# Attention scores as 64-query by 128-key products on quarters of the TensorE array, and a rearranged state-space stage (norm a turn ahead, B and C projected once, mask as a product)

## The reference

```python
x = x + ssd_block(layernorm(x))          # first stage: state-space attention in chunks, 4 heads of 64
x = x + layers(layernorm(x))             # 2 layers: local attention (8 heads of 64, window 64) and a gated feed-forward
x = x + scan_block(layernorm(x))         # selective scan, 256 channels x 16 states
x = x + layers(layernorm(x))             # the same 2 layers again
```

```python
# ssd_block
zxbcdt = u @ W_in.T                                   # z, x, B (16), C (16), dt (4 heads)
xBC = silu(conv(xBC, conv_w, 4 causal taps) + conv_b) # x 256, B 16, C 16 columns
Y[l] = sum over s <= l of (C[l] . B[s]) * exp(sum of A*dt from s+1 to l) * x[s] * dt[s]
y = rmsnorm((Y + x * D) * silu(z)) * norm_w;  return y @ W_out.T
# local attention in the layers
bk, bv = look_around(bk), look_around(bv)             # a window of 64 queries sees its own and the previous 64 keys
sim = einsum('bhwid,bhwjd->bhwij', bq, bk); mask = (i < j) | (i > j + WINDOW) | (j == -1)
out = einsum('bhwij,bhwjd->bhwid', softmax(where(mask, -inf, sim)), bv)
```

## Time and profile before

| what | value |
|---|---|
| time, median of 3 runs | 2699.14 us |
| profiled execution, its own time | 2696.49 us |
| its span | 2694.7 us |
| PE busy | 2297.0 us (85%) |
| DVE busy | 1937.9 us (72%) |
| ACT busy | 1874.6 us (70%) |
| POOL busy | 1522.5 us (57%) |
| mean granted clock of PE | 0.947 |
| first stage | 17.5 to 342.7 us |
| layers, first time | 352 to about 1105 us |
| scan | to about 1890 us |
| layers, second time | to the end |

### The profile page before, as it was taken

How to read it: one execution, slowest core, us unless ns; L and a number is a source line. 1 busy time by engine, 2 the same in 40 slices (tenths; PEclk the granted TensorE clock), 3 DMA queues, 4 the chain that set the end, 5 groups by cost and what they waited for, 6 DMA issues and landing times. The chain is left out here.

```text
span 2694.7 us, 46600 instructions
## 1 busy us (share of the span) xinstructions
PE 2297.0 (85%) x13516; PEld 1222.4 (45%) x13516; DVE 1937.9 (72%) x5318; ACT 1874.6 (70%) x4753; POOL 1522.5 (57%) x1356
## 2 busy tenths in 40 slices
PE   6999979999999999867776677667799999999997
PEld 3555535555555555412222222222355555555553
DVE  2332358777787777459988898999587777777774
ACT  3444348777787777577877787777577777777774
POOL 1222236656656566248876776777465656566552
PEclk9999979999999999978888888889999999999999
DMA  3000000000000000000000000000000000000000
GB/s 135 1 0 0 0 8 13 13 13 8 17 9 17 9 12 13 5 0 0 1 1 2 0 0 1 0 0 1 12 9 17 9 12 13 13 17 12 24 13 16
DMA packets 12191, 30.46 MB, mean 11 GB/s; under 512 B 2240, under 2 KB 2240, under 8 KB 11456
## 3 DMA queue, kind: packets, MB, share of 16 engines
q1 hardware_dynamic: 11968, 27.99, 3.7%
HBM read 9.11 MB, written 2.10 MB: 4 GB/s over the span
## 5 line engine op out<-in xcount | busy, mean ns | idle before, releaser
L496 POOL TENSOR_TENSOR arena<-arena 128x512 f32<-128x512 f32 x256 | 325.1, 1270 | 487.4 <-DVE arena L1457 487.4
L554 POOL TENSOR_TENSOR arena<-arena 128x512 f32<-128x512 f32 x256 | 328.7, 1301 | 125.7 <-ACT arena L1230 117.8
L502 POOL TENSOR_TENSOR arena<-arena,SR 128x512 f32<-128x512 f32 x256 | 272.7, 1065 | 81.1 <-ACT SR L1112 80.2
L905 PE MATMUL psum<-BS,tabs 96*128 96x512 bf16 x384 | 143.8, 435 | 202.0 <-DVE arena L1537 200.1
L1537 DVE TENSOR_TENSOR_SCAN arena<-arena,psum 128x512 f32<-128x512 f32 x256 | 311.0, 1215 | 3.2
L973 PE MATMUL psum<-arena,first 128*128 128x512 f32 x512 | 284.3, 644 | 12.1 <-POOL arena L545 11.8
L509 POOL TENSOR_TENSOR P<-P,RS 128x512 f32<-128x512 f32 x256 | 270.2, 1055 | 42.2 <-DVE RS L1384 42.1
L1463 DVE TENSOR_REDUCE SM<-arena 128x8 f32<-128x512 f32 x256 | 175.1, 684 | 156.3 <-ACT arena L1102 148.1
L1102 ACT ACTIVATE arena<-psum 128x512 f32<-128x512 f32 x256 | 151.3, 591 | 181.9 <-PE psum L831 181.3
L831 PE MATMUL psum<-rest,HA 128*128 128x512 f32 x512 | 266.6, 603 | 0.4 <-DVE HA L1372 0.4
L785 PE MATMUL psum<-HN,rest 128*128 128x512 f32 (+1 forms) x384 | 192.7, 628 | 33.3 <-ACT arena L1095 28.7
(11 more groups left out here) (220 smaller groups left out, 5795.9 us busy)
## 6 DMA issues: line engine op xcount, KB each, us to landing
arena<-arena SPq DMA_DIRECT2D x128, 128.0 KB, 2.3
rest<-in_rest SPq DMA_DIRECT2D x1, 4183.0 KB, 22.6
X<-in_x SPq DMA_DIRECT2D x1, 2048.0 KB, 10.6
out<-X SPq DMA_DIRECT2D x8, 256.0 KB, 2.2
first<-in_first SPq DMA_DIRECT2D x1, 1445.5 KB, 6.2
tabs<-in_tabs SPq DMA_DIRECT2D x1, 1216.0 KB, 13.1
```

The source lines that it names most:

```text
L496: nc.gpsimd.tensor_tensor(CQ[:, n % 2, :], CQ[:, n % 2, :], SQN[:, n % 2, :], ALU.add).then_inc(f_rope, 1)
L502: nc.gpsimd.tensor_tensor(heads, heads, SR[:, n % 2, :].unsqueeze(2).to_broadcast([128, HEADS, DH]), ALU.mult).then_inc(f_qk, 1)
L554: nc.gpsimd.tensor_tensor(WU[:, k % DEEP, :], RG[:, k % DEEP, :], U[t.j % 2][:, k % 2, :], ALU.mult).then_inc(m_wu, 1)
```

## The change

**First stage.** The layer norm runs a turn further ahead: turns go from -2 to 8 (`staged` in place of `pairs`, for this stage alone), turn j has mean and variance of pair j+2 (`a_pe_norm`, `a_act_norm`, `a_dve_norm`), in the STAT bank, and its square stands on POOL behind the decays. XN is made at h = 0 in place of h = 5, the positions of dt and the x projections move forward by three or four, x times dt goes from the end of the turn to the start of the next. B and C are projected by one 48-column product, and VectorE applies the four taps (`conv_bc`). The causal mask is no longer added in front of the exponential: VectorE multiplies each C-B product once by a table of ones and zeros into CBM. MM has four buffers, and two heads' outputs stand interleaved (`heads_out`). ScalarE's silus for B, C and z wait for the taps and stand at h = 12; its square of the norm is gone.

**Layers, both times.** The scores of two heads are 8 products of 64 queries by 128 keys, each on a quarter of the array, first half and then second half of the sequence. The second tile's layout of keys for the first 64 queries changes, and with it the `band` table and the halves of the mixed values. The wait for the scores' buffers stands ahead of the last product of `weigh`.

The core of the diff (left out: renumbered positions, semaphores, packing of `a_convw` and `a_convc`, ScalarE's positions):

```diff
-        convW = shared("ssd", [128, CONV, 304])
+        convW = shared("ssd", [128, CONV, 256])
+        win_bc = shared("ssd", [128, 48])
+        BCT = shared("ssd", [48, 2, SEQ])
+        CBM = shared("ssd", [128, 2, 384])
...
-        MM = shared("ssd", [128, 2, 384])
+        MM = shared("ssd", [128, 4, 384])
...
+                self.after = -1 <= j < PAIRS - 1
+                self.ahead = j < PAIRS - 2
...
+        def staged(eng, turn):
+
+            for j in (-2, -1, 0):
+                turn(Turn(eng, 0, j))
...
+                if t.ahead:
+                    t.wait_ge(ln_cen, 1, 1, pair=2)
+                    nc.gpsimd.tensor_tensor(LSQ[:, :], CEN[:, :], CEN[:, :], ALU.mult).then_inc(ln_sq, 1)
...
-                mm(seg[:, 0:384], T16("ident16"), T16("causal"), start=True, stop=False)
-                mm(seg[:, 0:128], AM[:, q % 2, 0, :], F("le"), start=False, stop=False)
-                mm(seg[:, 128:256], AM[:, q % 2, 0, :], F("ones"), start=False, stop=False)
-                mm(seg[:, 128:256], AM[:, q % 2, 2, :], F("le"), start=False, stop=False)
-                mm(seg[:, 256:384], AM[:, q % 2, 1, :], F("le"), start=False, stop=True).then_inc(a_seg, 1)
+                mm(seg[:, 0:128], AM[:, q % 2, 0, :], F("le"), start=True, stop=True)
+                mm(seg[:, 128:256], AM[:, q % 2, 0, :], F("ones"), start=True, stop=False)
+                mm(seg[:, 128:256], AM[:, q % 2, 2, :], F("le"), start=False, stop=True)
+                mm(seg[:, 256:384], AM[:, q % 2, 1, :], F("le"), start=True, stop=True).then_inc(a_seg, 1)
...
+            def heads_out(t, p):
+                b, h = divmod(2 * p, SSD_HEADS)
+                t.wait_ge(a_mm, 8, 2 * p + 2)
+                if p == 0:
                     t.wait_ge(a_xt, 4, 4)
                     t.wait_ge(a_yd, 2, 2, pair=-1)
-                y = Y_BANK[h // 2][64 * (h % 2):64 * (h % 2) + 64, :]
-                xh = XT[t.j % 2][:, :, DH * h:DH * h + DH]
-                mm(y[:, SEQ * b:SEQ * b + SEQ], xh[:, 2 * b, :], MM[:, q % 2, 0:256], start=True, stop=False)
-                mm(y[:, SEQ * b + 128:SEQ * b + SEQ], xh[:, 2 * b + 1, :], MM[:, q % 2, 256:384],
-                   start=False, stop=True).then_inc(a_y, 1)
+                both = [(Y_BANK[h // 2][64 * r:64 * r + 64, SEQ * b:SEQ * b + SEQ],
+                         XT[t.j % 2][:, :, DH * (h + r):DH * (h + r) + DH], MM[:, (2 * p + r) % 4, :]) for r in range(2)]
+                for y, xh, m in both:
+                    mm(y, xh[:, 2 * b, :], m[:, 0:256], start=True, stop=False)
+                for y, xh, m in both:
+                    mm(y[:, 128:256], xh[:, 2 * b + 1, :], m[:, 256:384], start=False, stop=True).then_inc(a_y, 1)
...
+            def a_pe_norm(t, h):
+                if h == 11:
+                    t.wait_ge(ln_log, 1, 1, pair=1)
+                    if t.before:
+                        t.wait_ge(a_x, 1, 1, pair=-1)
+                    mm(STAT, F("mean128"), X[:, t.tokens(2)], start=True, stop=True).then_inc(ln_mean, 1)
+                elif h == 14:
+                    t.wait_ge(ln_sq, 1, 1, pair=2)
+                    mm(STAT, F("mean128"), LSQ[:, :], start=True, stop=True).then_inc(ln_var, 1)
...
+                elif h == 8:
+                    t.wait_ge(a_act, 6, 1, pair=1)
+                    mm(X_BANK[0][0:48, :], win_bc[:, :], XN[:, :, 3:3 + SEQ], start=True, stop=True).then_inc(a_z, 1)
+                    t.wait_ge(a_act, 6, 2, pair=1)
+                    mm(X_BANK[1], F("a_win", 0, 128), XN[:, :, 3:3 + SEQ], start=True, stop=True).then_inc(a_z, 1)
                 elif h == 11:
-                    t.wait_ge(a_act, 6, 1, pair=1)
-                    conv(t, slice(256, 304), X_BANK[0][0:48, :], 0)
-                    conv(t, slice(256, 304), X_BANK[0][0:48, :], 2)
-                elif h == 12:
-                    t.wait_ge(a_act, 6, 2, pair=1)
-                    t.wait_ge(a_x, 1, 1, pair=-1)
-                    for half, dst in enumerate((X_BANK[1], STAT)):
-                        mm(dst, F("a_win", 128 * half, 128 * half + 128), XN[:, :, 3:3 + SEQ],
-                           start=True, stop=True).then_inc(a_z, 1)
+                    t.wait_ge(a_cv, 4, 4, pair=1)
+                    mm(X_BANK[0], F("a_win", 128, 256), XN[:, :, 3:3 + SEQ], start=True, stop=True).then_inc(a_z, 1)
...
-            def scores(k, m, g):
+            def wait_scores(k, m, g):
                 b, j = divmod(g, 4)
                 k.wait_ge(f_nb, 16, 2 * g, slot=m)
                 if j == 0:
                     k.wait_ge(f_qkt, 8, 4 * b + 4, slot=m)
+
+            def scores(k, m, g):
+                b, j = divmod(g, 4)
                 q, key = QKT[k.side(m)][:, j, :], QKT[k.side(m)][:, 4 + j, :]
                 halves = [(S_BANK[r], slice(64 * r, 64 * r + 64)) for r in range(2)]
-                at = SEQ * b
-                for s, rows in halves:
-                    mm(s[:, 0:128], q[rows, at:at + 128], key[rows, at:at + 128], start=True, stop=True)
-                for s, rows in halves:
-                    mm(s[:, 128:192], q[rows, at + 128:at + 256], key[rows, at + 128:at + 192], start=True, stop=True)
-                for s, rows in halves:
-                    mm(s[0:64, 192:256], q[rows, at + 128:at + 192], key[rows, at + 64:at + 128], start=True, stop=True)
-                for s, rows in halves:
-                    mm(s[64:128, 192:256], q[rows, at + 192:at + 256], key[rows, at + 192:at + 256],
-                       start=True, stop=True).then_inc(f_sim, 1)
+                first_key = SEQ * b
+                for tile in range(2):
+                    cols = slice(128 * tile, 128 * tile + 128)
+                    for window in range(2):
+                        at = first_key + 128 * tile + 64 * window
+                        seen = first_key + (64 + 64 * window if tile else 0)
+                        for s, rows in halves:
+                            last = mm(s[64 * window:64 * window + 64, cols], q[rows, at:at + 64], key[rows, seen:seen + 128],
+                                      start=True, stop=True)
+                            if tile and window:
+                                last.then_inc(f_sim, 1)
...
+                for r, (o, head, pt) in enumerate(halves):
+                    if r and following:
+                        wait_scores(k, *following)
...
+                        weigh(k, *k.heads(g - 1), k.heads(g + 2))
+                    elif k.heads(g + 2):
+                        wait_scores(k, *k.heads(g + 2))
...
+            def a_act_norm(t, h):
+                if h == 15:
+                    t.wait_ge(ln_var, 1, 1, pair=2)
+                    A(LLOG[:, :], STAT, ACT.Ln, bias=eps_col[:, :]).then_inc(ln_log, 1)
+                    t.wait_ge(ln_log, 1, 1, pair=2)
+                    A(LRS[:, :], LLOG[:, :], ACT.Exp, scale=-0.5).then_inc(ln_rs, 1)
...
+            def conv_bc(t, taps):
+                src = pair(X_BANK[0][0:48, :])
+                for i in taps:
+                    t.wait_ge(a_cv, 4, i, pair=1)
+                    if i == 0:
+                        t.wait_ge(a_act, 6, 4)
+                        t.wait_ge(a_z, 5, 3, pair=1)
+                        TS(BCT[:, :, :], src, F("a_convc", 3, 4, p=48), None, ALU.mult).then_inc(a_cv, 1)
+                    else:
+                        STT(BCT[:, :, i:], src[:, :, 0:SEQ - i], F("a_convc", 3 - i, 4 - i, p=48), BCT[:, :, i:],
+                            ALU.mult, ALU.add).then_inc(a_cv, 1)
+
+            def masked(t, b):
+                t.wait_ge(a_cb, 2, b + 1)
+                t.wait_ge(a_mm, 8, 4 * b + 4, pair=-1)
+                TT(CBM[:, b, :], CB_BANK[:, 0:384], T16("causal"), ALU.mult).then_inc(a_cm, 1)
+
+            def a_dve_norm(t, h):
+                if h == 12:
+                    t.wait_ge(ln_mean, 1, 1, pair=2)
+                    TT(CEN[:, :], X[:, t.tokens(2)], STAT, ALU.subtract).then_inc(ln_cen, 1)
+
+            def x_times_dt(t):
+                for tt in range(4):
+                    t.wait_ge(a_xtp, 2, tt // 2 + 1)
+                    at = 256 * (tt % 2)
+                    TT(XT[t.j % 2][:, tt, :].rearrange("p (h d) -> p h d", h=SSD_HEADS),
+                       X_BANK[1 - tt // 2][:, at:at + 256].rearrange("p (h d) -> p h d", h=SSD_HEADS),
+                       sp[:, 7, 4 * tt:4 * tt + 4].unsqueeze(2).to_broadcast([128, SSD_HEADS, DH]), ALU.mult).then_inc(a_xt, 1)
...
+                if h == 0:
                     t.wait_ge(ln_rs, 1, 1, pair=1)
                     t.wait_ge(ln_cen, 1, 1, pair=1)
                     t.wait_ge(a_z, 5, 5)
                     TT(XN[:, :, CONV - 1:], pair(CEN), pair(LRS), ALU.mult).then_inc(ln_out, 1)
...
             def a_dve_turn(t):
                 for h in range(16):
                     if t.states and h % 2 == 0:
                         q = h // 2
-                        t.wait_ge(a_cb, 2, q // 4 + 1)
+                        if h in (0, 2):
```

(16 more changed lines are left out.)

123 lines of the change are left out of this document (56 added, 67 removed).

## The result

The changed kernel takes **2673.32 us** (median of 4 runs, 2672.1 to 2681.07) against 2699.71 us before (4 runs): ratio **0.9909, interval 0.9892 to 0.9927**, 26 us less. Forecast were 2624 us, 2588 to 2652. The direction is right, a third of the gain came. The profiled execution took 2681.07 us (span 2679.3), 7.8 above its median, so the two profiles differ by 15 us where the medians differ by 26. The scan stage, which the change does not touch, is 6.9 us longer in this profile than in the one before.

A forecast was written before the change was run, and what follows sets the result against it. TensorE's queue was taken to bound the kernel. From the profiled 2696.5 us, 42.6 us for the first stage and 29 us for the layers were taken off, giving 2625, stated as 2624 us, range 2588 to 2652.

The forecast's parts named there:

- TensorE's work per turn: First stage, steady turn: work falls from 36.8 to 29.6 us through masks, B and C products and paired heads.
- Head pairs: First stage: two heads' outputs run together on column halves; four pairs of 0.79 us replace eight heads, saving 3.2 us per turn.
- New waits of a turn: First stage: TensorE waits 1.8 us for XN, 1.0 at the second z product, 1.4 lost at the end; turn 32.5 us.
- the 1.4 at the turn's end: First stage: 7.5 us chain behind segment sum 6 against TensorE's 6.1 us of work; 1.4 us lost per turn.
- rival 4: First stage: clock stays at 1.2 GHz, a turn's work doubles to 59 us; about 2815 us in total; chance 0.03.
- First turn, prologue, last turn: First stage outside steady turns: first turn saves 6.4 us, last turn with ending 4 us, work ahead of the turns loses 3.4.
- Scores of a group: Layers: four waves of four quarter-array products take 0.63 us per group, 0.24 us less than the old 0.87.
- Rival 3: Layers: weight loads bound the quarter products, a group takes 1.05 us; 2677 to 2700 us in total; chance 0.05.
- Groups that count: Layers: only groups 2, 3, 4 and 7 of eight gain, 0.9 us per slot, 29 us over 32 slots.
- 0.05 is lost: Layers, group 4: groups 3 and 4 want 0.48 of POOL's 0.49 us of room, hand-over takes 0.06; 0.05 us lost.
- Rival 2: First stage: POOL slows VectorE, or head pairs do not overlap; 3 us more per turn, 2645 to 2650 us; chance 0.14.
- Rival 1: Following engines speed up too: all 256 score groups count (61 us, not 29), turn waits shrink; 2592 us; chance 0.17.

The follow-up runs named there:

- e3: Changed kernel plus two unused products of 0.86 us each while TensorE waits for XN; 2656.92 us, ratio 0.9828 to the kernel before.
- e8: Changed kernel, VectorE making XN ahead of the previous pair's two operations, TensorE taking the two square products one step later; 2647.77 us, ratio 0.9833.
- e5: Changed kernel plus a VectorE memset of 64 columns ahead of the normalisation of HN in the layers; 2668.68 us, ratio 0.9898.
- e1: Changed kernel with the layers' new score products undone, so only the first stage is changed; 2678.07 us, ratio 0.9918.
- e4: Changed kernel plus four unused products while TensorE waits for the first gelu in the layers; 2702.96 us, ratio 1.0013.
- e6: Changed kernel plus two unused products while TensorE waits for the first gelu in the layers; 2663.64 us, ratio 0.9886.
- e11: Changed kernel plus a VectorE memset of 192 columns ahead of the normalisation of HN in the layers; 2671.03 us, ratio 0.9887.
- e12: Changed kernel with ScalarE's gelus ahead of the next group's exponentials in group 5, and VectorE's copy ahead of the reciprocals; 2704.49 us, ratio 1.002.
- e10: Changed kernel with e8's first stage, the 192-column memset before HN's normalisation and two unused products in the gelu wait; 2650.14 us, ratio 0.9831.
- e7: Changed kernel with VectorE making XN ahead of the two operations of the pair before, no fillers; 2649.57 us, ratio 0.9845.
- e14: Changed kernel with e8's first stage, the 192-column memset before HN's normalisation and one unused product in the gelu wait; 2640.21 us, ratio 0.9784.

## Why the prediction was wrong

The order of the waits and the mechanisms in the sum held. What failed is two terms: the lower clock behind a new pause, which was priced only for a whole stage, and the hold-up between POOL and VectorE in group 4, put at 0.05 us.

- *TensorE's work per turn.* 29.6 us forecast, 30.0 measured (e3, e8). Head pairs: 174.99 to 175.79 = 0.80 us a pair, as forecast. Right.
- *New waits of a turn.* XN 1.8 to 2.2, on average 1.95 (1.8 forecast; its own terms, 4.2 + 2 x 0.74 + 0.7 - 4.4, give 2.0), second z product 0.6 (1.0), the last pair 0.9 (the 1.4 at the turn's end). At full clock, with the XN wait filled, the turn is 33.3 us, 0.8 above the forecast: 5 us over six turns.
- *The step that failed: rival 4's price.* I let the lower clock count only if the stage stayed there for a third of its time, and argued from the layers, whose pauses of 1 us leave it at 1.00. (The stretch of the layers in rows 1 held none of the three falls that the same execution had behind such pauses, at 463, 1074 and 2617 us.) The new pause came out as forecast, 1.95 us for 1.8, and behind it each turn runs 3.4 or 6.8 us at 1.2 GHz: (35.65 - 33.3) x 6 = 14 us of the 19 missing in the steady turns. Filling the pause brought 17 us in the stage. This was a sure small loss, and I had priced an unlikely large one; the sign that I had named for it, a clock under 1.00 in the stage, came. The Trainium skill, TensorE: Matmul & The Clock Gate, section HAM oscillation, tells of a kernel whose waits let the clock fall once in every round of its loop; that is the pattern here, though its waits (about 3 to 5 us there) are longer than the 2 us of this trace, and it should have had a chance of its own.
- *First turn, prologue, last turn.* First turn -5.3 (forecast -6.4), prologue +4.8 (+3.4, with 6.8 us of low clock at its end), last turn with its ending -1.0 (-4). Of the last turn with its ending 16.7 us are at 1.2 GHz where 6.4 were; what that cost was not taken apart.
- *Scores of a group.* 0.63 us forecast, 0.60 measured. Rival 3 falls: four waves of 0.109 us with their loads hidden. (The 0.43 us of streaming in the old form count L732 and L734 once, since they start together.)
- *Groups that count.* Saving per slot 0.9 forecast, 0.39 measured. Groups 0, 1, 5 give nothing in sum, as forecast. The term that failed is that of group 4, "0.05 is lost": POOL's scaling was taken at its old 1.04 us, and VectorE, 0.3 us sooner against POOL than before, got in ahead of it: 0.48 us. With the order turned back (e5) the slot saves 0.75 us; against that stands the new wait of the flip for POOL, 0.41 us. Of the 29 us forecast for 32 slots the two passes of the profile show 5.2. Of the missing 24, 16 are the 0.51 us a slot just named, about 5 the clock (an estimate, 8 x 0.65), and 2 to 3 stay open. The clock: 27 us more at 1.2 GHz in the two passes, eight stretches of 3.4 us more, mostly behind the wait for the gelu, and a slot so hit is 0.65 us longer. In the slots shown that wait grew from 0.99 to 1.69 us (rows above and the earlier trace rows): 0.27 us because the faster scores reach it sooner, the rest because L882 no longer waits for POOL in group 5.
- *Rival 2* named the size, 3 us more per turn, but neither of its causes: the pairs overlap, and at full clock the turn is 0.8 us longer, not 3.
- *Rival 1* falls: the followers did not speed up; from the start of the projection to the product that waits for the gelu it is 5.24 us before (744.95 to 750.19) and after (725.21 to 730.45).

## What to carry to other kernels

A new wait of TensorE costs its length and then the slower products behind it: price both, per pause, also when the mean clock of the stage hardly moves. A pause that can't be avoided may be worth filling with unused products, but only as long as the shortest wait they stand in. When a fast part makes two engines' instructions meet in another order, look at which pairs work on SBUF at the same time; an instruction's old duration held here only beside its old neighbours.

## What the runs showed of the hardware

- **The clock falls behind a pause, not evenly.** All six pauses of 1.8 to 2.2 us in the steady turns were followed by 1.2 GHz, and 34 of 36 in the six other kernels with the same stage (e1, e4, e5, e6, e11, e12), the fall beginning in the pause or up to 2.0 us behind it. Of the waits of 1.7 to 2.0 us in the layers (idle 1.85 us, 728.60 to 730.45) 10 of 28 were, of the waits of about 1 us there before the change 3 of 28. Where it falls it stays for 3.4 or 6.8 us of busy products, and the same pause had either length from turn to turn. With XN first (idle time 0.3 to 0.7 us) the steady turns of e8 and e10 had none, those of e7 and e14 two, so a short pause makes a fall rarer and does not exclude it.
- **VectorE and POOL hold each other up whole.** Multiplications of two SBUF operands, 128x512: POOL 1.04 us when it starts first, 1.52 when 0.07 us late; VectorE 0.69 alone, 1.39 and 1.57 when POOL is ahead. The waiting one ends nearly its own duration after the other's end: VectorE 0.55 us behind POOL (719.73 + 1.04 = 720.77 and 721.32), POOL 0.90 us behind VectorE (722.04 and 722.94). The Trainium skill, SBUF — State Buffer, section SBUF: two separate sides, says the port that these two share is held for a whole instruction, and by the one that starts first; the rows agree in all 28 slots before and all 28 after, and do not in the slots of e11 where POOL starts 0.04 us ahead, behind a memset, and waits.
- **The scan stage is the noise.** Untouched in all kernels, it took 846.0 to 860.6 us in fourteen profiles, with 229 to 266 us at 1.2 GHz. Differences under some 5 us between single profiled executions say nothing; compare stretches.
